# Eight table stores issued by ScalarE, another way to spread a small number in a rare branch, and a weight load that waits for another

## The chip, the cores and the metric

The kernel runs on one core of one Trainium2 chip. The metric is the device time of one execution in microseconds (us), as the median of several runs. TensorE is PE in the profile's rows (PEld is its weight load), VectorE is DVE, ScalarE is ACT, GpSimd is POOL, SyncE is SP. SPq and ACTq are the DMA issues of SyncE and ScalarE.

## The reference

One layer of a graph transformer over 6250 nodes with 256 channels, in float32.

```python
xn = _layernorm(x)
x = x + _L0_gnn_ref(xn, ...) + _L0_mix_ref(xn[None], ...)[0]
x = x + _L0_ffn_ref(_layernorm(x)[None], ...)[0]
```

The first term gathers rows of `xt = xn @ weight` by the edge list and weighs four heads with a softmax. The second maps rows into a ball, makes q, k and v with one matrix, batch-normalises them, mixes them by small grouped matrices, and forms a linear attention:

```python
vk = jnp.einsum('ngdl,ngel->ngde', v, k)
out = jnp.einsum('ngde,ngdl->ngdl', vk, q)
out = out / (jnp.sum(v, -1, keepdims=True) + ATT_EPS)
```

There is one node for each position (L is 1 in that layout), so v stands above and below the fraction. It cancels unless it is so small that ATT_EPS counts, or the row was scaled down to the ball. The third term picks two of eight experts for the whole batch from the mean row, and runs 256 to 512 to 256 channels with both, followed by a layer norm.

## The kernel before

The 6250 rows are cut into 25 blocks of 250 tokens, 125 partitions by two tokens. All instructions are written out by hand per engine, each engine goes through its own list in order, and semaphores tie the lists together.

**First stage, the table (about 0 to 81 us).** SyncE issues the loads of x as eight groups of blocks (`LOADS`: 0, 1, 2, 3-4, 5-6, 7-9, 10-15 and 16-24; `load_x`), each as two DMAs (partitions 0-111 and 112-124), and then, for each block, waits for `xt_ready` and issues the store of that block's 264-column rows into the DRAM table `xt_table` (L454, two DMAs for a block). All of this is one DMA queue, SyncE's. DVE takes statistics of each block (`row_sums`, L1224), turns them into factors for five parts of the blocks (`PARTS`: 0-1, 2-4, 5-9, 10-15, 16-24; `row_square`, `row_clip`, `row_factors`, with two powers on GpSimd at L515 and L516 and two logarithms on ScalarE at L690 and L691), and makes the normed rows (`make_h`, L1284). Its list is fixed: for example row_sums(15), row_square(3), make_h(8), row_sums(16), make_h(9), row_sums(17), row_clip(3), row_sums(18), row_factors(3), make_h(10), and so on without PE up to row_square(4), row_clip(4), row_factors(4), make_h(16). PE transposes a block (L945) and, one step later, multiplies it (L957). ScalarE copies the transposed block (`keep_h`, L730) and the product (`keep_xt`, L738) into one of four buffers `xts`; for block 4 and later it first waits until the store of the block four before has landed:

```python
if t == 0 and b >= XS:
    act.wait_ge(xt_out[b % XS], 32 * uses(b - XS, XS))
```

ScalarE's step s holds keep_h(s), at s = 4, 8 and 14 the logarithms of parts 2 to 4, keep_xt(s - 1) and `later_load(s)`, whose DMAs are on ScalarE's own queue, from s = 8 on. (At s = 2 the logarithms of part 1 stand first.)

**Second stage (to 212 us).** PE multiplies all blocks by the q, k and v matrix, three times 25 groups (L978), ScalarE keeps them, DVE takes statistics; GpSimd gathers table rows once all stores have landed.

**Third stage (to 475 us).** Per block: the small matrices, the attention, norms, the output matrix. Here `divide_where_needed(b)` on DVE reads a flag which says that some v is tiny or some row's norm is large. Where the flag is set it divides as the reference does, with the small number eps taken per token. PE and ScalarE wait for `fixed`, which this function raises at its end. In the profiled execution the flag is set for one block, at 414.7 us. The branch makes eps for 125 x 2 tokens, widens it to 32 columns, transposes in 32 x 32 squares (the DVE transposes within such squares), and copies 16 times 32 x 64 so that each of the 128 partitions holds all 250 values of eps (L1579). Two adds (L1584), two reciprocals (L1587) and four products follow.

**Routing and experts (475 us to the end).** DVE works out the two experts. SyncE (for expert 0) and ScalarE (for expert 1) run `load_expert`, four DMAs each: first matrix w1, its bias b1, second matrix w2, its bias b2. SyncE then loads gamma and beta. `hidden(b)` on PE (L1182) multiplies by w1 of expert 0 (four groups f) and then of expert 1 (four groups); ScalarE applies the gelu with b1 (L916); `result(b)` (L1195) multiplies by w2, which DVE has scaled by the expert's weight (L1747).

Of the kernel before, what the change touches and what calls it, by code (L numbers as in the profile page):

```python
# [11 lines left out]
ALU = mybir.AluOpType  # L12
# [45 lines left out]
def gps_layer(nc, x, idx_dst, idx_src, w_gnn, attn_l, attn_r, w_qkv, bn_gamma, bn_beta, w_dw, w_pw,  # L58
# [43 lines left out]
    with ExitStack() as ctx:  # L102
        def sb(name, shape, dt=F32):
            return ctx.enter_context(nc.sbuf_tensor(name, shape, dt))
# [57 lines left out]
        et = sb("et", [128, 3, TB])  # L162
        ebt = sb("ebt", [128, 2, TB, 32])

# [9 lines left out]

        LW = 9914
        L = sb("L", [128, LW])

# [35 lines left out]
        spill = take(D // 2).bitcast(BF16)  # L213
        eb = take(BT)
        den = take(NH * BT)
# [177 lines left out]

        LOAD_AT, WQ_AT = 8, 15
        R_Q, R_K, R_V = 0, 1, 2
        KINDS = (R_K, R_Q, R_V)
# [31 lines left out]
        def load_x(eng, i):  # L428
            b0, b1_ = LOADS[i]
            for ph in HALVES:  # L430
                eng.dma_start(Z[ph, b0 * ZW:b1_ * ZW].rearrange("p (b n) -> p b n", n=ZW)[:, :, 0:XB],
                              xv[ph, b0:b1_]).then_inc(x_in[i], 16)

        def load_expert(eng, i):

            e = eng.value_load(chosen[0:1, i:i + 1], min_val=0, max_val=EX - 1)
            eng.dma_start(w1s[:, i, :, :], w1[e].rearrange("(k p) f -> p k f", p=128)).then_inc(w1_in[i], 16)
            eng.dma_start(b1s[:, i, :], b1[e].rearrange("(k p) -> p k", p=128),
                          allow_slow_non_contiguous=True).then_inc(b1_in[i], 16)
            eng.dma_start(w2s[:, i, :, :], w2[e].rearrange("(k p) f -> p k f", p=128)).then_inc(w2_in[i], 16)  # L440
            eng.dma_start(b2s[0:TP, i, :], b2[bass.ds(e, 1)].broadcast_to([TP, D])).then_inc(w2_in[i], 16)

        @block.sync
        def _(sp):
# [4 lines left out]

            for b in range(NB):  # L450
                a = b % XS
                sp.wait_ge(xt_ready.sem, xt_ready.count(b))
                for ph in HALVES:
                    sp.dma_start(xt_rows[ph, b], xts[ph, a].rearrange("p t d -> p (t d)")).then_inc(xt_out[a], 16)  # L454

# [42 lines left out]
        def _(pool):  # L498
# [5 lines left out]
            g.memset(chk[:, :, :].rearrange("p a c -> p (a c)"), 0.0).then_inc(const, 1)  # L504
            g.memset(ebt[:, :, :, :].rearrange("p a t c -> p (a t c)"), 0.0).then_inc(const, 1)
            g.iota(down[:], [[-1, EX]], base=EX, channel_multiplier=0,
# [162 lines left out]
        def _(act):  # L669
# [72 lines left out]
            for s in range(NB + 1):  # L742
# [7 lines left out]
                if s:  # L750
                    keep_xt(s - 1)
                later_load(s)
                if s == WQ_AT:
# [451 lines left out]
        def _(dve):  # L1205
# [350 lines left out]
            def divide_where_needed(b):  # L1556
# [12 lines left out]
                with dve.If(found > 0):  # L1569
# [3 lines left out]
                    alone(v_.tensor_scalar(et[0:TP, 2], et[0:TP, 1], ATT_EPS, None, ALU.mult))  # L1573
                    alone(v_.tensor_copy(ebt[0:TP, 0], et[0:TP, 2].rearrange("p (t a) -> p t a", a=1).broadcast_to([TP, TB, 32])))
                    alone(v_.transpose(ebt[:, 1].rearrange("p t c -> p (t c)"), ebt[:, 0].rearrange("p t c -> p (t c)")))
                    for q in range(4):
                        w = min(32, TP - 32 * q)
                        for p in range(4):
                            alone(v_.tensor_copy(eb.rearrange("p (t n) -> p t n", t=TB)[32 * p:32 * p + 32, :, 32 * q:32 * q + w],  # L1579
                                                 ebt[32 * q:32 * q + 32, 1, :, 0:w]), q == 3 and p == 3)  # L1580

                    halves = ((zc(b, 2 * R_V, 2), den, ob(b, 0, 2)), (ps[:, R_V, 0:2 * BT], vk, ob(b, 2, 2)))
                    for n, (v, d, _) in enumerate(halves):
                        alone(v_.tensor_tensor(pair(d), pair(v), eb.rearrange("p (a n) -> p a n", a=1)  # L1584
                                               .broadcast_to([128, NH, BT]), ALU.add), n == 1)
                    for n, (_, d, _) in enumerate(halves):
# [258 lines left out]
```

## Time and profile before

| | |
|---|---|
| median of 3 runs | 843.91 us (840.88 to 845.69) |
| the profiled execution | 845.02 us, of which the span from first to last instruction is 843.2 us |
| PE busy | 789.9 us, 94% of the span; mean granted clock 0.979 |
| DVE / ACT / POOL busy | 523.4 / 424.6 / 389.2 us |
| DMA moved | 41.32 MB, mean 49 GB/s |

The share of PE is an average. What a change is worth is read from where PE stands still, and from what ended that wait. Start times count from the start of the span.

### The profile page before, as it was taken

How to read it: one execution, taken by the hardware profiler on the slowest of the kernel's cores; microseconds unless marked ns; L12 is line 12 of the kernel's file. 1: busy time of each engine (PE TensorE's matmuls, PEld its weight loads, DVE VectorE, ACT ScalarE, POOL GpSimd, SP SyncE). 2: the span in 40 equal slices, each digit the busy share in tenths (PEclk: the TensorE clock that was granted, in tenths of full speed). 3: DMA queues.
4: the chain of work that ended last, by engine and by line, in shares of the span. 5: the costliest groups of instructions: out<-in, count | busy, mean ns of one | idle time of the engine just before them, and what ended most of it. 6: DMA issues, size and time to landing. Idle time of an engine off the chain costs nothing. (4 is left out here: it accounts for less than half of the span.)

```text
span 843.2 us, 15014 instructions
## 1 busy us (share of the span) xinstructions
PE 789.9 (94%) x5042; PEld 648.9 (77%) x5042; DVE 523.4 (62%) x1475; ACT 424.6 (50%) x959; POOL 389.2 (46%) x601
## 2 busy tenths in 40 slices
PE   5899999999799999999659889999999999999996
PEld 4678888888466667766436778888888888888885
DVE  7762488797578888788888643534444353535345
ACT  2466436889578888888647232323232323222230
POOL 2430778778068888887636601312222221312122
PEclk9899999999899999999969999999999999999999
DMA  9755122222011110211101040000000000000000
GB/s 213 192 152 152 40 58 56 55 52 52 8 48 43 55 57 25 64 42 51 45 7 33 19 125 13 17 21 22 16 25 13 24 13 25 13 25 14 25 20 30
DMA packets 35422, 41.32 MB, mean 49 GB/s; under 512 B 11520, under 2 KB 20696, under 8 KB 35339
## 3 DMA queue, kind: packets, MB, share of 16 engines
q1 hardware_dynamic: 22355, 30.71, 12.8%
q0 software_dynamic: 8000, 6.82, 3.8%
q10 hardware_dynamic: 4984, 2.79, 1.4%
q8 instruction: 40, 0.66, 0.3%
q14 instruction: 43, 0.35, 0.1%
HBM read 25.59 MB, written 14.60 MB: 48 GB/s over the span
## 5 line engine op out<-in xcount | busy, mean ns | idle before, releaser
L916 ACT ACTIVATE Z<-ps,b1s 128x250 f32<-128x250 f32 x200 | 93.5, 469 | 234.9 <-PE ps L1182 232.1
L1195 PE MATMUL ps<-Z 128*125 128x256 f32 x800 | 176.5, 379 | 0.0
L1182 PE MATMUL ps<-Z 128*128 128x250 f32 x800 | 173.6, 374 | 2.3 <-DMA Z<-in_w 2.3
L1195 PEld LDWEIGHTS ps<-Z 128*125 128x125 f32 x800 | 150.2, 188 | 22.2
L1182 PEld LDWEIGHTS ps<-Z 128*128 128x128 f32 x800 | 151.3, 189 | 20.5 <-DMA Z<-in_w 2.9
L978 PE MATMUL ps<-Z,L 128*128 128x250 f32 x600 | 126.9, 373 | 0.0
L651 POOL TENSOR_SCALAR zr<-zmv 125x1 f32<-125x1 f32 x50 | 11.1, 221 | 250.1 <-issue 240.3
L978 PEld LDWEIGHTS ps<-Z,L 128*128 128x128 f32 x600 | 113.6, 189 | 13.2
L1770 DVE TENSOR_TENSOR Z<-ps,L 125x256 f32<-125x256 f32 x50 | 21.2, 425 | 161.1 <-PE ps L1195 161.1
L1097 PE MATMUL ps<-wr,Z 128*125 128x256 f32 x400 | 92.6, 384 | 0.0
L774 ACT ACTIVATE Z<-Z,bn_o,bn_s 128x250 f32<-128x250 f32 x150 | 80.8, 600 | 1.5 <-DVE bn_o L1481 1.5
L1097 PEld LDWEIGHTS ps<-wr,Z 128*125 128x125 f32 x400 | 73.1, 188 | 9.8
L987 PE MATMUL ps<-Z,pw 64*64 64x250 f32 x600 | 55.4, 393 | 18.8 <-issue 17.7
L1362 DVE BATCH_NORM_STATS2 L<-Z 128x6 f32<-128x250 f32 x140 | 49.2, 409 | 27.8 <-ACT Z L770 27.7
L526 POOL DMA_INDIRECT L<-xt_table,idst x36 | 44.4, 1233 | 38.0 <-issue 37.2
L770 ACT ACTIVATE Z<-ps 128x500 f32<-128x500 f32 x75 | 43.5, 580 | 30.0 <-PE ps L978 29.4
L987 PEld LDWEIGHTS ps<-Z,pw 64*64 64x64 f32 x600 | 26.3, 136 | 39.7 <-issue 31.6
L957 PE MATMUL ps<-L,Z 128*125 128x264 f32 x200 | 53.1, 413 | 2.8 <-ACT Z L730 2.8
L529 POOL DMA_INDIRECT asrc<-xt_table,isrc x40 | 48.6, 1215 | 12.2 <-issue 12.2
L1075 PE MATMUL ps<-L,ones 128*32 128x250 f32 x600 | 49.5, 390 | 4.4 <-ACT L L801 4.2
L801 ACT ACTIVATE L<-ps 128x500 f32<-128x500 f32 x75 | 43.4, 586 | 9.7 <-PE ps L987 9.4
L1788 DVE SCALAR_TENSOR_TENSOR Z<-Z,zr 125x256 f32<-125x256 f32 x50 | 40.8, 815 | 9.7 <-POOL zr L653 6.5
(214 smaller groups left out, 1287.7 us busy)
## 6 DMA issues: line engine op xcount, KB each, us to landing
Z<-in_x SPq DMA_DIRECT2D x25, 250.0 KB
out<-Z SPq DMA_DIRECT2D x24, 250.0 KB
xt_table<-L SPq DMA_DIRECT2D x25, 231.0 KB
Z<-in_x SPq DMA_DIRECT2D x1, 2016.0 KB
g_table<-gt SPq DMA_DIRECT2D x25, 62.5 KB
gr<-g_table SPq DMA_DIRECT2D x25, 62.5 KB
Z<-in_x SPq DMA_DIRECT2D x1, 1344.0 KB
Z<-in_w SPq DMA_DIRECT2D x2, 512.0 KB, 3.4
```

The source lines that it names most:

```text
L526: g.indirect_dma_start(rows_at[:, t, :], None, xt_table, bass.IndirectOffsetOnAxis(ap=idst[0:TP, j:j + 1].bitcast(U32), axis=0)).then_inc( ...
L529: g.indirect_dma_start(left_at[:, t, :], None, xt_table, bass.IndirectOffsetOnAxis(ap=isrc[0:TP, j:j + 1].bitcast(U32), axis=0), element_o ...
L774: a_.activation(zc(b, c), zc(b, c), ACT.Relu, bias=bn_o[:, c:c + 1], scale=bn_s[:, c:c + 1]).then_inc(done.sem, 1)
L916: a_.activation(ge[:, b % 2, f, :], ps[:, f % 4, 0:BT], ACT.Gelu, bias=b1s[:, f // NF, f % NF:f % NF + 1]).then_inc(gelu_done.sem, 1)
L957: last = mm(ps[0:TP, 2 + 2 * (b % 2) + t, 0:XT], h_raw(b, k)[:, t * TP:(t + 1) * TP], wg[:, k, :], start=(k == 0), stop=(k == KD - 1))
L978: last = mm(ps[:, group_bank(n), h * BT:(h + 1) * BT], wq[:, k, c * 128:(c + 1) * 128], h_raw(b, k), start=(k == 0), stop=(k == KD - 1))
L987: return mm(to[cols_], lhsT[rows_, HALF * a:HALF * a + HALF], rhs[rows_], start=True, stop=True)
L1075: last = mm(ps[32 * q:32 * q + 32, 5, 0:BT], ones[:, 0:32], of, start=(i == 0), stop=(i == 3), skip_group_check=True)
L1097: last = mm(res_bank(b, t), ob(b, c, 1)[:, t * TP:(t + 1) * TP], wr[:, c, :], start=(c == 0), stop=(c == NO - 1))
L1182: last = mm(ps[:, f % 4, 0:BT], w1s[:, f // NF, k, (f % NF) * 128:(f % NF + 1) * 128], h_of(b, k), start=(k == 0), stop=(k == KD - 1))
L1195: last = mm(ps[0:TP, 4 + 2 * (b % 2) + t, 0:D], ge[:, b % 2, f, t * TP:(t + 1) * TP], w2s[:, f // NF, f % NF, :], start=(f == 0), stop=(f ...
L1362: v_.bn_stats(to, zc(b, c)).then_inc(z_sums.sem, 1)
```

## The change

Three edits. First, `store_xt(b)` of blocks 0 to 7 is issued by ScalarE at step s = b + 2, behind keep_xt(b + 1), on ScalarE's DMA queue; SyncE issues those of blocks 8 to 24. Second, in the branch eps is widened to 128 columns for each t in one copy, transposed as 128 x 256, and spread by two copies of 64 partitions and four of 32 partitions, each of 128 columns; the two adds read eps in another layout (h, t, n). The tile `ebt` and its clearing go, `den` is cleared instead, and `eb` grows from 250 to 256 columns. Third, SyncE waits for the landing of w1 of expert 1 before it issues w2 of expert 0; b2, gamma and beta stand behind that wait.

```diff
--- before.py
+++ after.py
@@ -160,7 +160,6 @@
         vr = sb("vr", [128, 2, TB])
         st2 = sb("st2", [128, TB, 6])
         et = sb("et", [128, 3, TB])
-        ebt = sb("ebt", [128, 2, TB, 32])
 
         b1s = sb("b1s", [128, TOP_K, NF])
         rt = sb("rt", [1, 19, EX + 1])
@@ -172,7 +171,7 @@
         zr = sb("zr", [128, 2, 2, 1])
 
 
-        LW = 9914
+        LW = 9920
         L = sb("L", [128, LW])
 
         def cut(base):
@@ -211,7 +210,7 @@
         vk = take(NH * BT)
         junk = take(BT).bitcast(BF16)
         spill = take(D // 2).bitcast(BF16)
-        eb = take(BT)
+        eb = take(TB * 128)
         den = take(NH * BT)
 
         take = cut((NB * XW, NB * ZW, Z))
@@ -392,6 +391,8 @@
         assert XS == 4 and EARLY % 2 == 0
 
         LOAD_AT, WQ_AT = 8, 15
+
+        EARLY_STORE = 8
         R_Q, R_K, R_V = 0, 1, 2
         KINDS = (R_K, R_Q, R_V)
 
@@ -431,12 +432,20 @@
                 eng.dma_start(Z[ph, b0 * ZW:b1_ * ZW].rearrange("p (b n) -> p b n", n=ZW)[:, :, 0:XB],
                               xv[ph, b0:b1_]).then_inc(x_in[i], 16)
 
+        def store_xt(eng, b):
+            a = b % XS
+            eng.wait_ge(xt_ready.sem, xt_ready.count(b))
+            for ph in HALVES:
+                eng.dma_start(xt_rows[ph, b], xts[ph, a].rearrange("p t d -> p (t d)")).then_inc(xt_out[a], 16)
+
         def load_expert(eng, i):
 
             e = eng.value_load(chosen[0:1, i:i + 1], min_val=0, max_val=EX - 1)
             eng.dma_start(w1s[:, i, :, :], w1[e].rearrange("(k p) f -> p k f", p=128)).then_inc(w1_in[i], 16)
             eng.dma_start(b1s[:, i, :], b1[e].rearrange("(k p) -> p k", p=128),
                           allow_slow_non_contiguous=True).then_inc(b1_in[i], 16)
+            if i == 0:
+                eng.wait_ge(w1_in[1], 16)
             eng.dma_start(w2s[:, i, :, :], w2[e].rearrange("(k p) f -> p k f", p=128)).then_inc(w2_in[i], 16)
             eng.dma_start(b2s[0:TP, i, :], b2[bass.ds(e, 1)].broadcast_to([TP, D])).then_inc(w2_in[i], 16)
 
@@ -447,11 +456,8 @@
                 if i == 1:
                     sp.dma_start(wg[:, :, 0:D], w_gnn.rearrange("(k p) d -> p k d", p=128)).then_inc(wg_in, 16)
 
-            for b in range(NB):
-                a = b % XS
-                sp.wait_ge(xt_ready.sem, xt_ready.count(b))
-                for ph in HALVES:
-                    sp.dma_start(xt_rows[ph, b], xts[ph, a].rearrange("p t d -> p (t d)")).then_inc(xt_out[a], 16)
+            for b in range(EARLY_STORE, NB):
+                store_xt(sp, b)
 
             def keep_g(b):
                 if b < EARLY:
@@ -502,7 +508,7 @@
             g.memset(nhalf[:], -0.5).then_inc(const, 1)
             g.memset(phalf[:], 0.5).then_inc(const, 1)
             g.memset(chk[:, :, :].rearrange("p a c -> p (a c)"), 0.0).then_inc(const, 1)
-            g.memset(ebt[:, :, :, :].rearrange("p a t c -> p (a t c)"), 0.0).then_inc(const, 1)
+            g.memset(den[:], 0.0).then_inc(const, 1)
             g.iota(down[:], [[-1, EX]], base=EX, channel_multiplier=0,
                    allow_small_or_imprecise_dtypes=True).then_inc(const, 1)
             pool.wait_ge(const, 7)
@@ -749,6 +755,8 @@
                         row_logs(i)
                 if s:
                     keep_xt(s - 1)
+                if 1 < s <= EARLY_STORE + 1:
+                    store_xt(act, s - 2)
                 later_load(s)
                 if s == WQ_AT:
                     act.wait_ge(wq_in, WQ_IN)
@@ -1571,18 +1579,25 @@
                     alone(v_.tensor_tensor(et[0:TP, 0], nrm[0:TP, a, :, 0], npw[0:TP, a, :, 0], ALU.mult))
                     alone(v_.tensor_scalar(et[0:TP, 1], et[0:TP, 0], 1.0 / A_MAX, 1.0, ALU.mult, ALU.max))
                     alone(v_.tensor_scalar(et[0:TP, 2], et[0:TP, 1], ATT_EPS, None, ALU.mult))
-                    alone(v_.tensor_copy(ebt[0:TP, 0], et[0:TP, 2].rearrange("p (t a) -> p t a", a=1).broadcast_to([TP, TB, 32])))
-                    alone(v_.transpose(ebt[:, 1].rearrange("p t c -> p (t c)"), ebt[:, 0].rearrange("p t c -> p (t c)")))
+
+
+
+                    alone(v_.tensor_copy(den[0:TP, 0:TB * 128].rearrange("p (t n) -> p t n", t=TB),
+                                         et[0:TP, 2].rearrange("p (t a) -> p t a", a=1).broadcast_to([TP, TB, 128])))
+                    alone(v_.transpose(eb, den[:, 0:TB * 128]))
+                    places = eb.rearrange("p (t q c) -> p t q c", t=TB, q=4)
+                    alone(v_.tensor_copy(places[64:128, :, 0:2], places[0:64, :, 0:2]), False)
+                    alone(v_.tensor_copy(places[0:64, :, 2:4], places[64:128, :, 2:4]))
                     for q in range(4):
-                        w = min(32, TP - 32 * q)
-                        for p in range(4):
-                            alone(v_.tensor_copy(eb.rearrange("p (t n) -> p t n", t=TB)[32 * p:32 * p + 32, :, 32 * q:32 * q + w],
-                                                 ebt[32 * q:32 * q + 32, 1, :, 0:w]), q == 3 and p == 3)
+                        p = q ^ 1
+                        alone(v_.tensor_copy(places[32 * q:32 * q + 32, :, p % 2:4:2], places[32 * p:32 * p + 32, :, p % 2:4:2]),
+                              q == 3)
+                    tokens = lambda a: a.rearrange("p (h t n) -> p h t n", h=NH, t=TB)
+                    eps = eb.rearrange("p (a t n) -> p a t n", a=1, t=TB)[:, :, :, 0:TP].broadcast_to([128, NH, TB, TP])
 
                     halves = ((zc(b, 2 * R_V, 2), den, ob(b, 0, 2)), (ps[:, R_V, 0:2 * BT], vk, ob(b, 2, 2)))
                     for n, (v, d, _) in enumerate(halves):
-                        alone(v_.tensor_tensor(pair(d), pair(v), eb.rearrange("p (a n) -> p a n", a=1)
-                                               .broadcast_to([128, NH, BT]), ALU.add), n == 1)
+                        alone(v_.tensor_tensor(tokens(d), tokens(v), eps, ALU.add), n == 1)
                     for n, (_, d, _) in enumerate(halves):
                         alone(v_.reciprocal(d, d), n == 1)
                     for n, (v, d, _) in enumerate(halves):
```

## Rows read from the trace of the kernel before

**Rows 1.** The page, the span in 40 equal slices of 21.1 us.

```profile
PE   5899999999799999999659889999999999999996
```

**Rows 2.** Timeline of PE, first stage: start, us, line, what, count [idle before].

```profile
36.10 3.55 PE L957 MATMUL ps<-L,Z 128*125 128x264 f32 x8 [2.82 <-ACT Z L730]
...
44.35 1.95 PE L957 MATMUL ps<-L,Z 128*125 128x264 f32 x8
...
58.83 0.65 PE L945 MATMUL ps<-ident,L 125*128 125x125 f32 x4 [1.48 <-DVE L L1284]
```

**Rows 3.** Timeline of ScalarE, first stage.

```profile
22.57 0.48 ACT L738 ACTIVATE L<-ps,L 125x264 f32<-125x264 f32 x1 [1.00 <-PE ps L957]
23.00 0.59 ACT L730 ACTIVATE Z<-ps 128x500 f32<-128x500 f32 x1
...
34.72 0.85 ACT L738 ACTIVATE L<-ps,L 125x264 f32<-125x264 f32 x2 [5.23 <-DMA xt_table<-L]
```

**Rows 4.** Timeline of DVE, first stage.

```profile
34.00 0.74 DVE L1224 BATCH_NORM_STATS2 L<-Z 125x6 f32<-125x256 f32 x2
...
36.37 0.69 DVE L1224 BATCH_NORM_STATS2 L<-Z 125x6 f32<-125x256 f32 x2
...
40.95 0.17 DVE L1265 TENSOR_TENSOR L<-L 125x12 f32<-125x12 f32 x1 [3.89 <-ACT L L691]
...
41.91 0.73 DVE L1284 TENSOR_SCALAR L<-Z,L 125x256 f32<-125x256 f32 x2
```

**Rows 5.** Timeline of GpSimd, first stage: the second power of part 3.

```profile
35.85 2.26 POOL L516 TENSOR_TENSOR L<-L,nhalf 125x12 f32<-125x12 f32 x1
```

**Rows 6.** Line L454, all stores of the table; ns min/median/max of one issue.

```profile
L454 SPq DMA_DIRECT2D xt_table<-L x50: 303/402/1517, 16.4 to 81.6; - x50
```

**Rows 7.** Windows of 2 us: engines' busy us, then PEclk, DMA share, GB/s.

```profile
24.00:26.00 2.00, 2.00 (x13) 1.71 (x12) 1.54 (x7) 1.59 (x5) 2.00 (x2) 1.00 1.06 228
...
32.00:34.00 2.00, 1.29 (x8) 0.87 (x6) 1.86 (x13) 0.00 (x0) 0.49 (x1) 1.00 0.73 215
...
46.00:48.00 2.00, 2.00 (x13) 1.71 (x12) 2.00 (x7) 1.36 (x3) 0.00 (x0) 1.00 1.01 273
```

**Rows 8.** Timeline of the branch, all engines.

```profile
415.27 0.20 DVE L1574 COPY ebt<-et 125x64 f32<-125x64 f32 x1
415.31 1.42 POOL L595 TENSOR_TENSOR Z<-Z,gr 125x256 f32<-125x256 f32 x2
415.50 0.24 DVE L1575 STREAM_TRANSPOSE ebt<-ebt 128x64 f32<-128x64 f32 x1
415.78 4.05 DVE L1579 COPY L<-ebt 32x64 f32<-32x64 f32 x16
...
430.44 0.65 PE L987 MATMUL ps<-Z,pw 64*64 64x250 f32 x1 [15.46 <-issue]
```

**Rows 9.** Groups by line and shape, DVE: busy us, mean ns; then L1579's own.

```profile
L1349 DVE COPY per<-raw 32x6 f32<-32x6 f32 x12 | 1.8, 152 | 5.2 <-DMA raw<-in_w_dw 4.9
...
L1354 DVE TENSOR_SCALAR pw<-pw,per 128x128 f32<-128x128 f32 x6 | 1.3, 280 | 0.0
...
L1579 DVE COPY L<-ebt x16: 184/186/651, 415.8 to 419.6; 32x64 f32<-32x64 f32 x12, 32x58 f32<-32x58 f32 x4
```

**Rows 10.** Timeline of routing and the first expert block; last, L437's landing.

```profile
489.57 0.45 SPq L440 DMA_DIRECT2D Z<-in_w  x1
489.61 0.44 ACTq L437 DMA_DIRECT2D Z<-in_w  x1
...
491.91 3.65 PE L1182 MATMUL ps<-Z 128*128 128x250 f32 x16 [0.28 <-DMA Z<-in_w]
...
497.56 3.65 PE L1182 MATMUL ps<-Z 128*128 128x250 f32 x16 [2.00 <-DMA Z<-in_w]
...
508.31 5.99 PE L1195 MATMUL ps<-Z 128*125 128x256 f32 x27
...
DMA to landing us min/median/max: 3.4/5.7/7.9
```

## Prediction

> **What bounds the kernel now.** I read the page's slices first [rows 1]. PE is at 9 of 10 nearly everywhere. Counted from 0, it is below that in slices 0 and 1, in 10, in 19 and 20, which hold the branch, and in 22 and 23, around routing. A change that takes work from another engine is worth something only where PE stands still, so for each edit I went to the timeline and looked for PE's idle time, what ended it, and whether another chain ends just behind.
>
> In the first stage PE has two idle times after 30 us: 2.82 us before 36.10, ended by ScalarE's copy, and 1.48 us before 58.83, ended by DVE's make_h(16) [rows 2]. The first goes back to ScalarE, which stood 5.23 us at keep_xt(4) for the landing of block 0's store [rows 3]: that store is queued behind all of x. From 58.83 on PE works on to the end of the second stage, so **the first stage's worth is decided at 58.83**. In the branch PE stands 15.46 us while DVE works alone [rows 8]. At the experts PE stands 2.00 us for w1 of expert 1 [rows 10].
>
> **Edit 1, stores on ScalarE.** The stall of 5.23 us goes. PE gains its 2.82 us and, as the next eight matmuls took 3.55 us instead of 1.95 at the lower of the two clock levels [rows 2], another 1.6 us; but only up to the next bound. make_h(16) hangs on a DVE list that runs without waiting for PE from make_h(10), at 41.91, on: statistics, two powers on GpSimd, factors. So the question is what moves 41.91. Before, it was the logarithms of part 3, which ScalarE could give only after its stall: DVE stood 3.89 us for them and restarted at 40.95 [rows 4]. Without the stall DVE's own list decides: row_sums(16), make_h(9), row_sums(17), row_clip(3), row_sums(18), which ran from 34.00 to 37.06, and 41.91 - 40.95 = 0.96 us of factors [rows 4]. So make_h(10) starts at T + 4.02, where T is when row_sums(16) can start, and the edit's worth at 58.83 is T + 4.02 - 41.91 = T - 37.9.
>
> row_sums(16) needs the last group of x loads. Before, nothing of the stores got ahead of x: the DMA engines were full to 32 us and at 0.73 from 32 to 34 [rows 7], and row_sums(16) started at 34.00 with no wait, so x landed shortly before. Now stores run beside x. ScalarE issues store 0 after 22.57 + 0.48 = 23.05, and one more per step. A step costs it 0.59 + 2 x 0.48 of copies [rows 3] and about 0.75 us for two issues (0.40 and 0.30, the median and minimum of [rows 6]), 2.3 us; with PE's own waits that puts stores 0 to 3 at about 23, 25.5, 28 and 32, and store 4 at 34. Each store is 264 KB; at the 228 GB/s that x was flowing at [rows 7] it takes 1.16 us of all 16 engines. Four of them push x from 34 to 34 + 4.6 = 38.6. Against this, where two queues ran together (46 to 48 us, weights and stores) the engines moved 273 GB/s at the same fill [rows 7]; at that rate the remaining 11 us of x and the 4.6 us of stores shrink by a sixth of themselves at most, some 2 us. Ends: T = 34.6 if x does not suffer (0.6 us because ScalarE's two issues push the logarithms of part 2), and T = 41 if six stores go ahead in full (34 + 6 x 1.16). I take 37.6, near the four-store value less half of the 2 us: **-0.3 us**, with ends -2.8 and +3.1. The first is held by GpSimd: its second power ended at 35.85 + 2.26 = 38.11 [rows 5], 0.6 later now, and 0.35 of factors follow, so make_h(10) cannot start before 39.1.
>
> DMAs pay for the move on each queue. SyncE loses 16 issues and nobody waits for it there. On ScalarE 16 issues of 0.3 to 0.4 us cost about 6 us in a stretch where it had waited; behind them stand keep_h and the logarithms. From step 10 on no store is left on it, and its step of 1.55 us is below PE's, whose eight matmuls alone take 1.95 [rows 2]. Clearing `den` (500 columns) in place of `ebt` (128) on GpSimd lies at the kernel's start, where PE still waits for its first weights: nothing.
>
> The page DMA: Bandwidth & Descriptors of the Trainium skill, sections Queues, rings and completion order and Issuing engines are not separate DMA queues, says that all issuing engines feed the same 16 DMA engines, which take their queues in turn packet by packet, so that a second issuer brings no bandwidth. By this rule x pays for every store in full, which is the second rival below, at T = 39.3; the row at 273 GB/s is why I don't go all the way.
>
> **Edit 2, the branch.** Removed: from 415.27 to 415.78 + 4.05 = 419.83, 4.56 us, that is one copy, one transpose and 16 copies [rows 8]. The copies go out without waits between them, one in about 0.22 us for a duration of 0.186, but two beside GpSimd's add took 0.32 and 0.65 [rows 8, 9]. Added: a copy of 256 columns, a transpose of 256 columns, six copies of 128 columns. Copies took 152 ns for 6 columns and 186 for 64 [rows 9], 0.6 ns a column, so 0.23 us for 128 and 0.30 for 256; the slowest like row is L1354, 0.28 for 128. The transpose took 0.24 for 64; with 1 ns a column it is 0.44, if it grows in proportion 0.98. Sum: 0.30 + 0.44 + 6 x 0.26 + three gaps of 0.06 = 2.5, and 0.6 more for GpSimd's add, which runs until 416.73: 3.1. Ends: 2.5 (no disturbance) and 3.7 (transpose in proportion). The adds have the same 500 columns in another order: nothing. I take **-1.5 us** (4.56 less the sum; ends -0.9 and -2.1). All of it lies on the path, because PE and ScalarE stand still throughout; the flag was set for one block only.
>
> **Edit 3, w2 behind w1.** w1 of expert 1 was issued at 489.61, beside w2 of expert 0 at 489.57 on the other queue, and landed 7.9 us later, where w1 of expert 0 took 3.4 us [rows 10]. Its 0.5 MB alone need the time that w1 of expert 0 took, so it lands between 493.0 (3.4 us) and 495.5. PE is through with expert 0's groups at 491.91 + 3.65 = 495.56: the 2.00 us go. Late next is w2 of expert 0, with b2, gamma and beta behind SyncE's wait: issued at about 495.4, 5 to 6 us to land, then 2.4 us of scaling on DVE, so about 504. PE needs it for result(0), at 508.31 - 2.0 = 506.3 [rows 10]. Covered by 2 us; without this cover each us late would be a us lost. **-2.0 us** (0 to -2.0).
>
> **Sum.** -0.3 - 1.5 - 2.0 = -3.8 us. Against the profiled execution: 845.02 - 3.8 = 841.2, its span 843.2 - 3.8 = 839.4. The profiled execution is 1.1 us above the median; from 843.91 it gives **840.1 us**. Half a per cent, 4.2 us, is about what a measurement of this kernel can tell from no change (its three runs lie 4.8 us apart), so this is just inside.
>
> **Rivals.**
>
> *x does not suffer.* The stores fit into gaps, T = 34.6: edit 1 gives -2.8. For it: 273 GB/s with two queues. Against: DMA share 1.06 while x loads [rows 7]. Sum -6.3: 837.6 us.
>
> *x pays in full.* T = 39.3, edit 1 costs +1.4, sum -2.1: 841.8 us. For it: w1 of expert 1 took 7.9 us beside another queue [rows 10]. Against: only stores issued early enough count.
>
> *A lower clock at block 16.* PE reaches turn_h(16) earlier than DVE, and its idle time before 58.83 grows from 1.48 to about 2.5 us. After 2.82 us of idle the next eight matmuls ran at the lower level and cost 1.6 us; after 1.48 they did not [rows 2]. Sum -2.2: 841.7 us.
>
> *The experts' load stays slow.* If w1 of expert 1 is held by something other than w2, for example the many small pieces of b1, edit 3 gives 0: sum -1.8, 842.1 us.
>
> *Slower: the stores starve x.* Six stores go ahead of the last x group, T = 41, +3.1; DVE is late, PE stands before blocks 9, 10 and 16 and runs twice at the lower level, +3.2. With edits 2 and 3: +2.8, 846.7 us. It decides from T = 41 on; against it, ScalarE itself stops at step 8 for part 3, so it cannot issue store 6 before T.
>
> **How the numbers follow.** Forecast 0.38; x does not suffer 0.22; x pays in full 0.14; lower clock 0.12; slow expert load 0.09; slower 0.05. The range that leaves out 2 in 10 runs from 836.8, just past the first rival, to 843.6, past the slow expert load. Faster by over 0.5%: all of the first rival and half of the forecast's spread, 0.41; slower 0.05; the rest 0.54.
>
> **What would show it.** Edit 1: no wait of ScalarE at L738 for xt_table; DVE's L1224 waits for x at about 34 to 38; make_h(10) near 41.6 and PE at make_h(16) near 58.5. If make_h(10) is at 39, the first rival holds. Edit 2: the first add 3.1 us after the wide copy's start, PE's idle 14.0 instead of 15.46. Edit 3: L1182 runs from expert 0 to 1 without a wait, w2 not waited for at L1195. The prediction is wrong if the block-16 gate isn't what holds PE, or if the lower clock level appears in places where it wasn't.

## The result, and the profile after

| | before | changed |
|---|---|---|
| median of 5 runs | 842.66 us (840.88 to 845.69) | 838.03 us (837.54 to 839.38) |
| the profiled execution, its span | 845.02 us, 843.2 us | 839.38 us, 837.5 us |

The ratio of the times is 0.9938 with a 95% interval of 0.9915 to 0.9962: 0.6% faster, 4.6 us by the medians. The prediction was 840.1 us within 836.8 to 843.6; the time lies in the range, 2.1 us below the forecast. In a second series the changed kernel ran at 838.95 us beside 842.62, ratio 0.9950 (0.9931 to 0.9968).

The two profiled executions differ by more, 5.7 us. The page of the changed kernel, its 40 slices of 20.9 us:

```profile
PE 788.3 (94%) x5042; PEld 648.4 (77%) x5042; DVE 522.5 (62%) x1465; ACT 424.5 (51%) x959; POOL 389.3 (46%) x601
...
PE   4999999999799999999669899999999999999996
```

Against [rows 1] the slices look alike: the change is in idle times of one to three microseconds, and those are read in the timelines. PE in the first stage (start, us, line, what, count [idle before]):

```profile
41.90 2.04 PE L965 MATMUL ps<-L,Z 128*125 128x264 f32 x8 [0.69 <-ACT Z L736]
...
56.67 0.65 PE L953 MATMUL ps<-ident,L 125*128 125x125 f32 x4 [1.67 <-DVE L L1292]
57.15 1.95 PE L965 MATMUL ps<-L,Z 128*125 128x264 f32 x8
```

The 2.82 us stand of [rows 2] before 36.10, with its eight matmuls at the lower level, is gone, and block 16 starts at 56.67 instead of 58.83: -2.16 us. ScalarE, with its stores now its own (ACTq rows are its DMA issues):

```profile
23.08 1.19 ACTq L439 DMA_DIRECT2D xt_table<-L  x2
...
32.30 0.48 ACT L744 ACTIVATE L<-ps,L 125x264 f32<-125x264 f32 x1 [1.60 <-DMA xt_table<-L]
...
34.22 0.48 ACT L744 ACTIVATE L<-ps,L 125x264 f32<-125x264 f32 x1 [0.45 <-DMA xt_table<-L]
```

The wait for the table has shrunk from 5.23 us [rows 3] to 1.60 + 0.45, but it is still there: store 0 was issued at 23.08 and block 4 waited for its landing until 32.30, 9.2 us for 264 KB. DVE:

```profile
35.20 0.75 DVE L1232 BATCH_NORM_STATS2 L<-Z 125x6 f32<-125x256 f32 x2
...
39.43 0.17 DVE L1280 SCALAR_TENSOR_TENSOR L<-L 125x12 f32<-125x12 f32 x1 [0.68 <-POOL L L522]
...
39.77 0.73 DVE L1292 TENSOR_SCALAR L<-Z,L 125x256 f32<-125x256 f32 x2
```

row_sums(16) starts at 35.20 and doesn't wait for x; GpSimd's second power is waited for 0.68 us; make_h(10) starts at 39.77, not 41.91 [rows 4]. The branch:

```profile
412.52 0.29 DVE L1585 COPY L<-et 125x256 f32<-125x256 f32 x1
412.56 1.57 POOL L601 TENSOR_TENSOR Z<-Z,gr 125x256 f32<-125x256 f32 x2
412.85 0.45 DVE L1587 STREAM_TRANSPOSE L<-L 128x256 f32<-128x256 f32 x1
413.33 0.22 DVE L1589 COPY L<-L 64x128 f32<-64x128 f32 x1
413.58 0.63 DVE L1590 COPY L<-L 64x128 f32<-64x128 f32 x1
...
414.25 0.97 DVE L1593 COPY L<-L 32x128 f32<-32x128 f32 x4
415.25 0.68 DVE L1600 TENSOR_TENSOR L<-Z,L 128x500 f32<-128x500 f32 x1
...
425.83 0.65 PE L995 MATMUL ps<-Z,pw 64*64 64x250 f32 x1 [13.29 <-issue]
```

From the wide copy to the first add it is 2.73 us. Before, the copies' end stood 4.56 us behind the start [rows 8] and the first add 4.60. PE's idle time fell from 15.46 to 13.29 us. The experts:

```profile
487.38 3.65 PE L1190 MATMUL ps<-Z 128*128 128x250 f32 x16 [0.25 <-DMA Z<-in_w]
...
491.72 0.37 SPq L449 DMA_DIRECT2D Z<-in_w  x1
...
491.75 3.65 PE L1190 MATMUL ps<-Z 128*128 128x250 f32 x16 [0.73 <-DMA Z<-in_w]
...
496.83 1.42 DVE L1762 TENSOR_SCALAR Z<-Z,tw 128x1024 f32<-128x1024 f32 x2 [0.85 <-DMA Z<-in_b]
...
502.50 0.81 PE L1203 MATMUL ps<-Z 128*125 128x256 f32 x3
```

PE stands 0.73 us for w1 of expert 1, where it stood 2.00 [rows 10]; SyncE issues w2 of expert 0 at 491.72, the moment that w1 has landed. result(0) at 502.50 doesn't wait: the cover held.

So the 5.7 us are: 2.16 in the first stage, about 0.6 in the 350 us between block 16 and the branch (branch start 412.52 against 415.27, 2.75 ahead), 1.87 in the branch, 1.27 at the experts; what is left, -0.2, is scatter. The sum of the three edits is 5.3 us, and it seems to close. The experiments ask whether the first term is the edit's.

### The profile page after: what moved, and what is told of

Its sections match the earlier page's. It is cut to its first block and busy times, and to the rows that moved or that the text cites. A ratio compares the mean times of both kernels' runs of the same rounds, so it can differ in the third digit from the quotient of the medians.

```text
span 837.5 us, 15004 instructions
## 1 busy us (share of the span) xinstructions
PE 788.3 (94%) x5042; PEld 648.4 (77%) x5042; DVE 522.5 (62%) x1465; ACT 424.5 (51%) x959; POOL 389.3 (46%) x601
## 5 line engine op out<-in xcount | busy, mean ns | idle before, releaser
L995 PE MATMUL ps<-Z,pw 64*64 64x250 f32 x600 | 54.6, 387 | 16.2 <-issue 16.2
L995 PEld LDWEIGHTS ps<-Z,pw 64*64 64x64 f32 x600 | 26.2, 134 | 36.8 <-issue 30.0
```

The source lines that it names most:

```text
L995: return mm(to[cols_], lhsT[rows_, HALF * a:HALF * a + HALF], rhs[rows_], start=True, stop=True)
```

## Experiments

Ratios are against the kernel before on the same chip. Its median was 842.58 us beside the first four runs, 842.62 beside the last four. The four with one execution each (e5 to e8) ran beside one execution of it, at 840.07 us, so that their traces are read and their times are not compared.

### One edit undone at a time

**e1_noA**, the changed kernel with all stores on SyncE:

```diff
-        EARLY_STORE = 8
+        EARLY_STORE = 0
...
-                if 1 < s <= EARLY_STORE + 1:
+                if EARLY_STORE and 1 < s <= EARLY_STORE + 1:
```

> The changed kernel with all table stores back on SyncE; edits 2 and 3 stay. In the two traces PE reached make_h(16)'s block 2.16 us earlier after the change. Theory 1 (edit 1 is worth what that shift says and it is kept to the end): this run is 2.2 us slower than the changed kernel, about 840.2, and 2.5 us (0.3%) faster than before. Rival (the shift is given back later, or the whole gain of 5 us is a gain of the other two edits): no slower than the changed kernel, 838. In its trace: ScalarE's wait for xt_table of about 5.2 us is back, and PE's restart at block 16 is at 58.8.

**e2_noB**, the branch as before, the other two edits kept:

```diff
-                    alone(v_.transpose(eb, den[:, 0:TB * 128]))
...
+                    alone(v_.transpose(ebt[:, 1].rearrange("p t c -> p (t c)"), ebt[:, 0].rearrange("p t c -> p (t c)")))
                     for q in range(4):
+                        w = min(32, TP - 32 * q)
+                        for p in range(4):
```

> The changed kernel with the branch as before (ebt, one transpose of 64 columns, 16 copies); edits 1 and 3 stay. Theory 1: PE's idle time in the branch goes from 13.3 back to about 15.2 to 15.5 us, and the time is 1.9 us above the changed kernel, about 839.9. Rival (the other kernels' timing around the branch shifts as the phase does, so that the two traces' difference is not the edit's): a difference under 1 us.

**e3_noC**, without the wait before w2:

```diff
-            if i == 0:
-                eng.wait_ge(w1_in[1], 16)
```

> The changed kernel without SyncE's wait before w2 of expert 0; edits 1 and 2 stay. Theory 1: PE's wait for w1 of expert 1 goes from 0.73 back to 2.0 us, and the time is 1.3 us above the changed kernel, 839.3. Rival (w2 late costs something at the first result that the wait gives back): under 0.5 us.

| kernel | median, runs | ratio | 95% interval |
|---|---|---|---|
| e1_noA (edits 2, 3) | 840.3 us, 12 | 0.9974 | 0.9955 to 0.9994 |
| e2_noB (edits 1, 3) | 839.35 us, 12 | 0.9957 | 0.9940 to 0.9974 |
| e3_noC (edits 1, 2) | 839.85 us, 12 | 0.9966 | 0.9949 to 0.9982 |

(One of the 12 executions of e1_noA took 4639 us; why is not known, and nothing here rests on it.) Each is slower than the changed kernel, but by 1 to 3 us with intervals as wide, so the times alone don't rank the edits. The 840.3 us of e1_noA is what its first theory named, under which edit 1 is worth 2.2 us; its trace isn't, and it speaks against the first term. Without the early stores its timelines show:

```profile
33.29 0.85 ACT L744 ACTIVATE L<-ps,L 125x264 f32<-125x264 f32 x2 [3.69 <-DMA xt_table<-L]
...
34.67 2.05 PE L965 MATMUL ps<-L,Z 128*125 128x264 f32 x8 [1.28 <-ACT Z L736]
...
55.87 0.65 PE L953 MATMUL ps<-ident,L 125*128 125x125 f32 x4 [1.47 <-DVE L L1292]
56.35 1.95 PE L965 MATMUL ps<-L,Z 128*125 128x264 f32 x8
```

ScalarE's stall is 3.69 us and not 5.23, PE loses 1.28 us and not 2.82, its next eight matmuls keep the higher level, and block 16 starts at 55.87: earlier than in the changed kernel. The first stage of e1_noA is that of before but for one clearing on GpSimd, so the 58.83 of before was not what this code gives each time. Two rows account for the 2.96 us between the two: ScalarE's wait ended at 34.72 instead of 33.29, 1.43 us later, and behind PE's longer idle time the next eight matmuls took 3.55 us [rows 2] instead of 2.05, 1.50 more. What let store 0 land later is not known.

In e2_noB the branch's numbers are those of before within a hundredth (PE's idle 15.46 us):

```profile
411.55 0.20 DVE L1582 COPY ebt<-et 125x64 f32<-125x64 f32 x1
411.78 0.25 DVE L1583 STREAM_TRANSPOSE ebt<-ebt 128x64 f32<-128x64 f32 x1
412.06 4.05 DVE L1587 COPY L<-ebt 32x64 f32<-32x64 f32 x16
416.14 0.68 DVE L1592 TENSOR_TENSOR L<-Z,L 128x500 f32<-128x500 f32 x1
...
426.72 0.65 PE L995 MATMUL ps<-Z,pw 64*64 64x250 f32 x1 [15.46 <-issue]
```

### Where w1 of expert 1 spends its time

With the wait, w1 of expert 1 still took 6.7 us to land where the prediction had 3.4 to 5.9. **e4_w2_late** asks whether w2 of expert 1, on ScalarE's queue right behind it, slows it: both w2 go out on SyncE after w1 of expert 1 has landed.

```diff
             if i == 0:
                 eng.wait_ge(w1_in[1], 16)
-            eng.dma_start(w2s[:, i, :, :], w2[e].rearrange("(k p) f -> p k f", p=128)).then_inc(w2_in[i], 16)
-            eng.dma_start(b2s[0:TP, i, :], b2[bass.ds(e, 1)].broadcast_to([TP, D])).then_inc(w2_in[i], 16)
+                load_second(eng, 0, e)
+                eng.wait_ge(rt_dve, RT_SECOND)
+                load_second(eng, 1, eng.value_load(chosen[0:1, 1:2], min_val=0, max_val=EX - 1))
```

> The changed kernel, but the second matrices and second biases of both experts are issued by SyncE once w1 of expert 1 has landed. The w1 of expert 1 took 6.7 us after the change although w2 of expert 0 was held back. Theory (the w2 of expert 1, right behind it on ScalarE's queue, moves at the same time and delays its landing): w1 of expert 1 lands 4 to 5.5 us after its issue, PE's wait of 0.73 us goes, 0.7 us faster than the changed kernel, 837.3; the w2s land by about 498, before PE wants them at 502. Rival (the 512 small pieces of each b1 in front of it delay it): still 6 to 7 us, and no gain. If the w2s come late, PE waits at the first result and the time rises.

837.96 us in 7 runs, ratio 0.9945 (0.9921 to 0.9969): the same as the changed kernel. w1 of expert 1 landed after 6.3 us, where the theory had 4 to 5.5, and PE's wait was 0.39 us. So w2 alone isn't it. Windows of half a microsecond (engines' busy us, then PEclk, DMA share, GB/s) show what is:

```profile
488.50:489.00 0.50, 0.50 (x4) 0.46 (x3) 0.00 (x0) 0.49 (x2) 0.00 (x0) 1.00 0.90 280
489.00:489.50 0.50, 0.50 (x4) 0.46 (x3) 0.00 (x0) 0.50 (x3) 0.00 (x0) 1.00 0.47 31
489.50:490.00 0.50, 0.50 (x4) 0.43 (x4) 0.00 (x0) 0.36 (x2) 0.00 (x0) 1.00 0.06 12
490.00:490.50 0.50, 0.50 (x4) 0.46 (x3) 0.00 (x0) 0.34 (x1) 0.00 (x0) 1.00 0.06 25
490.50:491.00 0.50, 0.47 (x3) 0.08 (x1) 0.00 (x0) 0.13 (x1) 0.00 (x0) 1.00 0.07 13
```

The bulk is through before 489.5. From there to 491.0 the share is 0.06 or 0.07, one sixteenth: what one busy engine of the 16 would give, moving 12 to 25 GB/s, and PE's matmuls on w1 start only at 491.36. The Trainium skill's page DMA: Bandwidth & Descriptors, section Why a DMA increments its semaphore by 16 and not by 1, says that a DMA runs on up to 16 engines that finish independently, each adding one to the semaphore behind its own data, and that only the full 16 means that all has landed; the kernel waits for 16, and this trace agrees: PE starts behind the last sixteenth part, at 491.36.

**e8_b1_early** asks whether the many small pieces of b1 are what that engine works on:

```diff
-            eng.dma_start(b1s[:, i, :], b1[e].rearrange("(k p) -> p k", p=128),
-                          allow_slow_non_contiguous=True).then_inc(b1_in[i], 16)
...
                 if n == 15:
+                    for i in range(TOP_K):
+                        act.dma_start(b1s[:, i, :], b1[i].rearrange("(k p) -> p k", p=128),
+                                      allow_slow_non_contiguous=True).then_inc(b1_in[i], 16)
```

> The changed kernel with the first bias of experts 0 and 1 loaded early in the first stage instead of those of the two chosen experts after routing, so the bias is that of fixed experts and the output differs. Theory (b1's 512 small pieces in front of the large loads delay w1 of expert 1): it lands 3.5 to 5 us after issue instead of 6.7, and PE's wait of 0.73 us goes. Rival (w2 of expert 1 behind it does): still above 6 us.

w1 of expert 1 took 7.2 us and PE waited 1.32 us, with b1 out of the way; in the last half microsecond before it the share is again a sixteenth:

```profile
492.50:493.00 0.50, 0.00 (x0) 0.00 (x0) 0.00 (x0) 0.00 (x0) 0.00 (x0) 1.00 0.07 18
...
493.27 3.65 PE L1191 MATMUL ps<-Z 128*128 128x250 f32 x16 [1.32 <-DMA Z<-in_w]
```

So it isn't b1 alone either; no run took out both. One rival was left untested, and the traces let it stand. In all 14, one packet of a queue named instruction moves while w1 of expert 1 loads. In e4_w2_late, from 487.5 to 488.5 us (queue: packets, MB, share of 16 engines):

```profile
q8 instruction: 1, 0.02, 9.4%
```

9.4% of 16 engines over 1 us are 1.5 us of one engine; over the 14 traces it is 0.9 to 1.8 us, and the tail here is about as long. The packet comes 2.0 to 3.5 us after the issue of w1 in twelve traces, and 4.0 us after it in two, e6_probe_after and e9_store4; those two have the shortest landings, 4.8 and 5.3 us. Whether it lay on the engine that was late, the traces don't show.

### Does x pay for the early stores

GpSimd idles at this time. In three kernels it waits for x groups 6 and 7, the last, and clears one column at the moment when they have landed:

```diff
+                if i == 3:
+                    for j in (6, 7):
+                        pool.wait_ge(x_in[j], 32)
+                        g.memset(probe[:, j:j + 1], 0.0)
```

**e5_probe_before** is the kernel before with it, **e6_probe_after** the changed one:

> The kernel before, with two probes: GpSimd, ahead of its powers of part 3, waits for the x groups 10-15 and 16-24 and clears one word after each. The second clearing shows when the last x group has landed: between 30.6 (all bytes moved on average) and 34.0. If it is after 33.5 it holds up the powers by as much.

> The same two probes in the changed kernel. Theory 1 (stores on a second queue hardly delay x, since also before the engines that were through with x moved stores behind it): the last group lands within 0.7 us of the run with probes before. Rival (x pays, but DVE came to row_sums(16) late enough, at 35.2, to hide it): it lands 1.5 us or more later, between 34.5 and 35.2. The first x group of the two (10-15) lands at the same time in both, as the first store is issued only at 23.1.

**e7_double** is the changed kernel with it and with blocks 0 to 3 stored twice by ScalarE, the second time into a spare table, 1.06 MB more:

```diff
+            if b < 4:
+                for ph in HALVES:
+                    eng.dma_start(spare_rows[ph, b], xts[ph, a].rearrange("p t d -> p (t d)")).then_inc(spare_out[b], 16)
```

> The changed kernel with the probes, and with blocks 0 to 3 stored twice by ScalarE, the second time into a spare table that nobody reads (1.06 MB more on ScalarE's queue; block b + 4 waits for both). Theory 1: the last x group lands less than 1 us later than in the run with probes alone; the stores themselves land later, so ScalarE's wait for xt_table grows by 3 us or more. Rival (shared alike): x lands 3 to 4.6 us later, at 37 or more, and DVE's row_sums(16) waits for it.

One row each, in this order, from the timelines of GpSimd:

```profile
32.78 0.10 POOL L517 MEMSET probe<- 128x1 f32 x1 [5.79 <-DMA Z<-in_x]
```

```profile
35.28 0.10 POOL L523 MEMSET probe<- 128x1 f32 x1 [8.45 <-DMA Z<-in_x]
```

```profile
32.67 0.10 POOL L529 MEMSET probe<- 128x1 f32 x1 [5.47 <-DMA Z<-in_x]
```

The last x landed at 32.78 us, at 35.28 with the early stores, and at 32.67 with the early stores and 1.06 MB beside them. The second value is the one that e6_probe_after's rival named, and DVE stood there for x, as in no trace without the edit:

```profile
35.26 0.75 DVE L1237 BATCH_NORM_STATS2 L<-Z 125x6 f32<-125x256 f32 x2 [1.39 <-DMA Z<-in_x]
```

The third value goes against e7_double's rival: 1.06 MB at 228 GB/s [rows 7] are 4.6 us, and x landed no later. The three executions differ before ScalarE has issued any store, though. This is what SyncE's queue had moved by 22.00 us, in the same order (packets, MB, share of 16 engines). Stores stand behind x on it or, with the edit, elsewhere; with all of x it comes to 6.66 MB:

```profile
q1 hardware_dynamic: 2705, 4.83, 91.8%
```

```profile
q1 hardware_dynamic: 2551, 4.52, 90.7%
```

```profile
q1 hardware_dynamic: 2750, 4.92, 91.1%
```

The 1.83, 2.14 and 1.74 MB that were left took 10.78, 13.28 and 10.67 us, that is 170, 161 and 163 GB/s. At 170 GB/s the 0.31 MB by which e6_probe_after was behind are 1.8 of the 2.5 us, and the stores cost x about 0.7 us there and 0.4 us in e7_double. These are estimates from one execution of each. So x seems to pay, but little beside the forecast's 3.6 us: row_sums(16) starts at 34.05 to 35.40 in the nine traces with eight or four early stores, at 33.95 to 34.34 in the four without, and DVE waits for x in three of the nine (0.30, 0.77 and 1.39 us).

What pays more is the store, which lands 9.2 us after its issue. e7_double's expectation that ScalarE's wait for the table would grow by 3 us or more was missed as well: it is 1.37 us. Its windows of 1 us show the engines full at 355 and 359 GB/s, a rate that no window of [rows 7] reaches.

```profile
29.00:30.00 1.00, 0.00 (x0) 0.00 (x0) 0.93 (x5) 0.24 (x1) 0.00 (x0) 1.00 1.01 359
30.00:31.00 1.00, 0.73 (x6) 0.69 (x7) 1.00 (x4) 0.05 (x1) 0.00 (x0) 1.00 0.99 355
```

The best microsecond of the four kernels without the edit, between 24 and 32 us, has 311 to 332 GB/s; in the changed kernel, e6_probe_after and r3_onlyA it has 365, 406 and 400. The Trainium skill's page DMA: Bandwidth & Descriptors, sections Queues, rings and completion order and Issuing engines are not separate DMA queues, lets the queues take turns by packets on the same engines. The traces agree that stores move while x does; that x is late by all of their bytes, as the prediction's second rival had it, the landings don't show.

### Is the first edit worth anything

**r3_onlyA** is the kernel before with edit 1 alone, **r1_after_again** and **r2_noA_again** repeat the changed kernel and e1_noA on one chip, and **e9_store4** gives ScalarE four stores:

```diff
-        EARLY_STORE = 8
+        EARLY_STORE = 4
```

> The changed kernel once more, on the chip of the next three. 0.994 of before again if its first measurement holds (837.5 to 838.5 beside 842.6).

> The changed kernel with all table stores on SyncE, once more. Its first profile had PE at block 16 at 55.87, earlier than the changed kernel's 56.67, although its median was 2.3 us longer. Theory A (edit 1 is worth 2 to 3 us in the median): 2 to 3 us above the changed kernel of the same call. Theory B (edit 1 is worth next to nothing; the 2.16 us between the first two traces was how fast x flowed in those two executions): within 1 us of it.

> The kernel before with edit 1 alone. Theory A: 0.9965 to 0.9975 of before, 2 to 3 us. Theory B: 0.999 to 1.001. Its profile gives one more value of PE's start at block 16: with stores on ScalarE this was 55.4 to 57.2 in six executions, with stores on SyncE 55.9, 56.2 and 58.8.

> The changed kernel with only the stores of blocks 0 to 3 on ScalarE. Edit 1's cost is ScalarE's issues at 0.75 us a block, of which four go; its use is over when x has landed, before store 4 is due. If the issues on ScalarE cost time, this is 0.3 to 1 us faster than the changed kernel; if they lie in idle time, the same within 0.5 us. If store 4 on SyncE's queue still lands late, ScalarE's wait at block 8 shows it.

| kernel | median, runs | ratio | 95% interval |
|---|---|---|---|
| r1_after_again (edits 1, 2, 3) | 838.95 us, 10 | 0.9950 | 0.9931 to 0.9968 |
| r2_noA_again (edits 2, 3) | 839.25 us, 12 | 0.9956 | 0.9937 to 0.9975 |
| r3_onlyA (edit 1) | 843.03 us, 12 | 0.9997 | 0.9980 to 1.0014 |
| e9_store4 | 838.04 us, 7 | 0.9940 | 0.9919 to 0.9960 |

Edit 1 alone is worth 0.3 us by its ratio, between 1.7 gained and 1.2 lost. With and without it beside the other two the ratios are 0.9950 and 0.9956 here; in the first series they were 0.9938 and 0.9974. Over both series, beside medians of the kernel before of 842.6 to 842.7 us, the 15 executions with all three edits average 838.8 us and the 23 with edits 2 and 3 alone 839.7 us (the one of 4639 us left out). That is 0.9 us, with an interval of about 0 to 2. So edit 1 is worth between nothing and 2 us, and most of the gain is that of edits 2 and 3. Four stores do as well as eight. No kernel here beats the changed one by more than the intervals.

Why it is worth so little stands at block 16, over all 14 profiled executions. The last column is the start of PE's first group of eight 64*64 matmuls in the repeating steps (L995), a point that all kernels share.

| execution | edit 1 | block 16 starts | idle before | next 8 matmuls | steps start |
|---|---|---|---|---|---|
| before | no | 58.83 | 1.48 | 1.95 | 214.89 |
| e1_noA | no | 55.87 | 1.47 | 1.95 | 211.99 |
| r2_noA_again | no | 55.80 | 1.50 | 1.95 | 211.81 |
| e5_probe_before | no | 56.24 | 1.49 | 1.95 | 212.38 |
| changed | yes | 56.67 | 1.67 | 1.95 | 212.76 |
| r1_after_again | yes | 56.86 | 2.62 | 1.95 | 213.00 |
| e2_noB | yes | 56.25 | 2.65 | 3.40 | 214.08 |
| e3_noC | yes | 56.72 | 2.62 | 2.82 | 214.44 |
| e4_w2_late | yes | 56.97 | 2.58 | 3.11 | 214.72 |
| e6_probe_after | yes | 57.19 | 2.63 | 2.87 | 215.02 |
| e8_b1_early | yes | 55.44 | 2.62 | 3.24 | 214.05 |
| r3_onlyA | yes | 55.94 | 2.65 | 3.63 | 214.56 |
| e9_store4 | 4 stores | 55.91 | 2.63 | 3.19 | 213.66 |
| e7_double | yes, twice | 58.79 | 1.85 | 1.95 | 214.87 |

Without the edit three of four start block 16 near 56.0; the profiled execution of before is the odd one, late by 2.6 to 3.0 us. With it they start there too, at 55.4 to 57.2. In all 14 traces block 16 starts 16.9 us behind make_h(10), so the question is what holds make_h(10). Without the edit it is ScalarE's logarithms of part 3. With it DVE waits for GpSimd's second power in four traces (0.29 to 0.70 us), for x in e9_store4, and in e2_noB, e3_noC, e4_w2_late and r3_onlyA again for the logarithms (0.73 to 1.07 us), because ScalarE now stands in its own issues just ahead of them. In r3_onlyA:

```profile
35.09 2.08 ACTq L439 DMA_DIRECT2D xt_table<-L  x2
37.22 0.59 ACT L734 ACTIVATE Z<-ps 128x500 f32<-128x500 f32 x1 [1.65 <-issue]
```

PE began to transpose block 8 at 34.89 there, 1.66 us earlier than in e1_noA, but the two issues took 2.08 us and keep_h(8) came at 37.22; in e1_noA it came at 37.18. In the other three the same two issues took 1.87 to 2.28 us.

At block 16 itself PE comes sooner and stands longer for make_h(16). In seven of the nine traces with eight or four stores the extra microsecond of idle has a price that the shorter one hasn't. r3_onlyA once more, PE's timeline and windows of 2 us:

```profile
55.94 0.65 PE L951 MATMUL ps<-ident,L 125*128 125x125 f32 x4 [2.65 <-DVE L L1290]
56.42 3.63 PE L963 MATMUL ps<-L,Z 128*125 128x264 f32 x8
```

```profile
54.00:56.00 2.00, 0.07 (x1) 0.07 (x2) 1.21 (x5) 0.42 (x1) 0.27 (x1) 1.00 0.55 166
56.00:58.00 2.00, 2.00 (x8) 1.67 (x9) 2.00 (x7) 0.59 (x1) 0.00 (x0) 0.62 0.03 8
58.00:60.00 2.00, 2.00 (x6) 1.35 (x6) 0.46 (x2) 0.48 (x1) 0.00 (x0) 0.53 0.00 0
60.00:62.00 2.00, 2.00 (x13) 1.75 (x12) 0.74 (x2) 1.52 (x4) 0.00 (x0) 1.00 0.31 78
```

After an idle time of 2.65 us the granted clock is 0.62 and 0.53 for four microseconds, near the lower of the levels of 1.2 and 2.4 GHz, and six to eight matmuls fit into two microseconds instead of twelve or thirteen. From block 16 to the start of the steps it is 156.0 to 156.1 us in the four executions without the edit, and 157.7 to 158.6 in the seven with a slow group behind block 16: the price is 1.6 to 2.5 us. In two of the nine with eight or four stores (the changed kernel's and r1_after_again's) the clock stayed up, in the second after the same idle time of 2.62 us; what decides it is open. These nine traces average 214.0 us at the start of the steps, the four without 212.8; the times of many runs don't show that microsecond as a loss, and single profiles scatter by three, so I take the loss no further than "not a gain".

## Why the prediction was right, and where it wasn't

**What bounds the kernel.** Right. The places where time moved are the four idle times that it listed, but for 0.6 us between block 16 and the branch, and the first stage's worth is decided at block 16.

**Edit 1, -0.3 us (-2.8 to +3.1).** Measured -0.3 (-1.7 to +1.2) in r3_onlyA, and -0.9 (about -2 to 0) over both series beside the other edits: the size is about right, its working is not, and that is luck. The formula held where DVE's list or GpSimd decides: with T = 35.20 it gives make_h(10) at 39.22, and the trace has 39.77, held by GpSimd's second power as foreseen. The failed steps are four.

- "The stall of 5.23 us goes": 0 to 2.2 us of it stay, because a store issued at 23 us lands at 32 (the changed kernel's).
- "Four of them push x from 34 to 38.6", from which T was taken as 37.6: T was 34.05 to 35.40, and the estimate of what x pays is 0.4 to 0.7 us.
- "Without the stall DVE's own list decides": in four of nine traces the logarithms still did, as two issues on ScalarE took 1.87 to 2.28 us just ahead of them, where the prediction had 0.75 us.
- The start, 58.83, was taken from one execution, which was 2.6 to 3.0 us later there than three others of the same code.

So the rival *x does not suffer* was nearest on T (34.6), and its -2.8 seemed confirmed by the first pair of traces (-2.16); most of that is the excess of one profile over its own kind. It was the rival *a lower clock at block 16* that took gain back: its growth of idle from 1.48 to about 2.5 us is what was measured (2.62), and its +1.6 us is 1.6 to 2.5. It was given 0.12 and came in seven of nine. Two slips in the working are of no weight: a sixth of 15.6 us is 2.6, not 2, and 38.6 + 0.6 is 39.2, not 39.3.

**Edit 2, -1.5 us (-0.9 to -2.1).** Measured -1.87 from the wide copy's start to the first add (4.60 to 2.73), -2.17 in PE's idle time, in every trace with the edit (13.28 to 13.31 us against 15.46). The terms: wide copy 0.30, measured 0.29; transpose 0.44, measured 0.45, so its time grows by 1 ns a column over a fixed part; the six copies with their gaps and 0.6 for GpSimd's add were 2.3 and came out at 1.9 (413.33 to 415.25). The one copy beside the add took 0.63 as against 0.22 for its twin, so the disturbance was 0.4, not 0.6. PE's idle time came to 13.29 us where 14.0 was named. By the runs, e2_noB's 0.9957 against 0.9938 and 0.9950 gives 1.6 and 0.6 us, with intervals as wide as this.

**Edit 3, -2.0 us (0 to -2.0).** Mis-sized, with the forecast set at the end of its own range: -1.27 in the first two traces. PE's wait for w1 of expert 1 was 2.00, 1.80, 2.21 and 1.55 us in the four traces without the wait before w2 (mean 1.9), and 0.73, 0, 0.54, 0.98, 0.67, 0, 1.12 and 0 in eight with it and nothing else changed there (mean 0.5): -1.4 us. The step that failed is that w1 "lands between 493.0 (3.4 us) and 495.5", after 3.4 to 5.9 us; it took 4.8 to 7.0. Where the windows were read without another load behind it, in e4_w2_late, its last sixteenth part ended about 1.5 us behind the rest. The direction was right, since without the wait it took 7.5 to 8.2, and so was the cover for w2. Not foreseen: an idle time of 2.21 us, in r3_onlyA, drops the clock here too, so that the wait is worth more than its length when it is long:

```profile
495.47 5.33 PE L1188 MATMUL ps<-Z 128*128 128x250 f32 x16 [2.21 <-DMA Z<-in_w]
```

against 3.65 us for the same 16 elsewhere, +1.7. With e3_noC's ratio against the changed kernel's two the edit is worth 1.4 to 2.4 us.

**Sum.** -3.8 was forecast; by the traces' own terms over many executions it is about 0, -1.9 to -2.2 and -1.4, together -3.3 to -3.6, and the two timed comparisons gave -4.6 and -3.7 by the medians. The forecast stood on a median of 843.91 for the kernel before; with five runs it is 842.66, and this 1.25 us is more than half of the 2.1 us between forecast and result. The 0.62% gained is on the faster side of the half per cent that was called the limit of what can be told, and its interval (0.38% to 0.85%) lies on both sides of it: the two nearly equal chances, 0.41 and 0.54, describe that well.

**Open.** Why x is 0.3 MB further at 22 us in one execution than in another, why two issues on ScalarE take 2 us at times, why the clock stays up after 2.62 us in one trace and falls in seven others, and what holds the DMA engine that ends w1 late.

## What to carry to other kernels

A gain that two traces seem to show is tested by undoing the one edit and looking at the stage again: here most of 2.16 of 5.7 us was one profile's lateness, and three more profiles of the same code were enough to see it. Moving DMA issues to an engine puts them ahead of that engine's next work: ask who waits for that work, and price the slow issue, not only the median one. Removing a stall ahead of a bound only makes the engine arrive sooner; if it then stands longer than before in one piece, PE's clock can take the gain back, so ask how long the next idle time becomes, not only whether there is one. A copy chain in which nothing else can run is worth shortening by instruction count, since its price is so many instructions by a duration that depends little on their width.

## What the runs showed of the hardware

With a second queue at work the full DMA engines moved 359 to 406 GB/s in their best microseconds, in four traces, where the four traces with one queue had at most 311 to 332; the 264 KB store of the second queue still took 9.2 us in the changed kernel. Two issues on ScalarE took 0.7 to 0.8 us mostly, and up to 2.28 us. A 0.5 MB load ended on what its share says is one of 16 engines, about 1.5 us after the others, at 12 to 25 GB/s (e4_w2_late). One packet of the instruction queue held 0.9 to 1.8 us of one DMA engine's time. PE's eight matmuls at block 16 ran at the higher level behind all six idle times of 1.47 to 1.85 us, and at the lower behind seven of the eight of 2.58 to 2.65 us.
